# Tokenise, mix, route: the mixing loop of a three-stage model with router logits taken from unnormalised rows

## The reference, cut to what matters

```
h = tok(x)                                  # 16 sequences x 255 tokens x 256
h = h + attn(layernorm(h))                  # gated linear recurrence over tokens
h = h + ffn(layernorm(h))                   # 8 experts, top 1
# in ffn, with y = layernorm(h) (mean and variance over 256, eps 1e-5):
wg_n   = wg / max(norm(wg), 1e-4)
logits = (y @ w_red) @ wg_n.T               # 8 per token
gates  = softmax(logits); pick argmax; out = expert(y) * score
```

## Time and profile before

| what | value |
|---|---|
| median of 3 runs | 721.15 us (720.75 to 727.15) |
| the profiled execution | 719.72 us |
| its span | 718.0 us |
| PE, DVE, ACT, POOL busy | 86%, 67%, 33%, 29% of the span |
| mean granted TensorE clock | 0.905 of full |

### The profile page before, as it was taken

How to read it: one execution, slowest core, us unless ns; L and a number is a source line. 1 busy time by engine, 2 the same in 40 slices (tenths; PEclk the granted TensorE clock), 3 DMA queues, 4 the chain that set the end, 5 groups by cost and what they waited for, 6 DMA issues and landing times. The chain is left out here.

```text
span 718.0 us, 12918 instructions
## 1 busy us (share of the span) xinstructions
PE 614.3 (86%) x3301; PEld 397.0 (55%) x3302; DVE 481.7 (67%) x1258; ACT 239.5 (33%) x475; POOL 209.7 (29%) x293
## 2 busy tenths in 40 slices
PE   3989999999999999999619988899327999999993
PEld 3757776666677776666314444444113565665652
DVE  2568888888888888888658778784582444444441
ACT  2124444434434444434410222222202333333430
POOL 7322222222222222122111112121042455554532
PEclk8999999999999999999965779796556999999998
DMA  9101110111111100110012223211001212222210
GB/s 253 38 30 59 59 42 16 58 58 58 58 58 58 58 30 29 58 59 29 30 39 89 68 68 91 86 51 37 23 1 44 59 61 63 61 62 62 64 49 0
DMA packets 30309, 39.85 MB, mean 56 GB/s; under 512 B 5090, under 2 KB 21731, under 8 KB 30288
## 3 DMA queue, kind: packets, MB, share of 16 engines
q1 hardware_dynamic: 21712, 26.04, 12.0%
q0 software_dynamic: 3744, 9.34, 4.5%
q10 hardware_dynamic: 4832, 4.21, 1.9%
HBM read 30.92 MB, written 9.59 MB: 56 GB/s over the span
## 5 line engine op out<-in xcount | busy, mean ns | idle before, releaser
L465 PE MATMUL banks<-proj,xnT_h 128*128 128x512 f16 x384 | 114.4, 379 | 13.8 <-DVE early L1055 13.8
L1492 POOL TENSOR_TENSOR sm<-sm,minus_half 128x1 f32<-128x1 f32 x64 | 40.9, 639 | 124.7 <-DVE sm L1026 83.4
L465 PE MATMUL banks<-proj,xnT_l 128*128 128x512 f16 x192 | 72.8, 379 | 0.0
L465 PEld LDWEIGHTS banks<-proj,xnT_h 128*128 128x128 f16 x384 | 36.3, 98 | 55.9 <-DVE early L1055 17.6
L1391 DVE TENSOR_TENSOR vo<-banks,vo 128x256 f16<-128x256 f32 x39 | 16.6, 425 | 70.9 <-ACT vo L871 70.9
L1572 POOL DMA_INDIRECT out<-proj,vo x39 | 39.6, 1016 | 79.7 <-DVE vo L1408 79.7
L440 PE MATMUL banks<-early 128*128 128x256 f32 x256 | 62.0, 385 | 0.7 <-ACT early L728 0.7
L442 PE MATMUL banks<-early 128*128 128x256 f32 x256 | 60.5, 379 | 0.0
L1496 POOL TENSOR_TENSOR w1l<-stage,w1h 128x512 f32 (+1 forms) x16 | 18.5, 1156 | 140.6 <-ACT w1h L772 140.6
L671 PE MATMUL banks<-w2h,vo 128*128 x312 | 57.5, 273 | 1.2 <-DVE proj L1406 1.2
L651 PE MATMUL banks<-w1h,vo 128*128 x156 | 55.0, 394 | 3.2 <-ACT vo L877 2.1
(11 more groups left out here) (258 smaller groups left out, 1370.4 us busy)
## 6 DMA issues: line engine op xcount, KB each, us to landing
early<-in_x SPq DMA_DIRECT2D x16, 512.0 KB, 4.3
stage<-in_W SPq DMA_DIRECT2D x32, 256.0 KB, 2.8
early<-lam_by_chunk SPq DMA_DIRECT2D x32, 132.0 KB
token_rows<-rows ACTq DMA_DIRECT2D x16, 129.0 KB, 2.3
token_rows<-rows ACTq DMA_DIRECT2D x16, 112.9 KB, 1.9
early<-in_tok_W SPq DMA_DIRECT2D x2, 512.0 KB, 8.4
early<-lam_by_head SPq DMA_DIRECT2D x16, 64.0 KB
vo<-token_rows,vo POOLq DMA_INDIRECT x39, 2.9
```

The costliest lines, as they stand in the source:

```text
L465: last = mm(dst, a, c, start=(i == 0), stop=(i == n - 1))
L1492: ptt(sm[:, dst:dst + 1], sm[:, src:src + 1], minus_half[:], ALU.pow).then_inc(s["rstd_ready"], 1)
```

## The change

The router weights are centred in the prologue (one `bn_stats`, `bn_aggr` and subtraction on 16 partitions instead of a plain copy). In the mixing loop the residual sum goes to a ring `h2` of four rows of 258 instead of back into `rows`; PE transposes the unnormalised row and makes the logits with tokens on partitions, all 32 tiles side by side in bank 0; `normalise2`, `turn_logits`, `keep_logits` and `collect_logits` are gone. POOL does three operations for each tile (variance plus epsilon, and the power twice: once to `rstd2`, once behind the row). The routing starts with one multiplication of all logits by `rstd2`. The order of PE and of ACT inside a slot is changed as well, and the ring adds waits on the stores and transposes of four tiles earlier.

```diff
             def logits(t, w):
                 pe.wait_ge(s["t2_evac"], t + 1)
                 for c in range(DC):
-                    last = mm(banks[0:E, 0, 0:P], wrg[:, c, :], xT2[:, w, c * P:c * P + P], start=(c == 0), stop=(c == DC - 1))
+                    last = mm(banks[:, 0, bass.ds(t * E, E)], xT2[:, w, c * P:c * P + P], wrg[:, c, :],
+                              start=(c == 0), stop=(c == DC - 1))
                 last.then_inc(s["lg_ready"], 1)
...
-            def transpose_xn2(t, w):
-                pe.wait_ge(s["xn2_ready"], t + 1)
+            def transpose_h2(t, k):
+                pe.wait_ge(s["h2_done"], t + 1)
...
             def pair(p, ahead=True):
                 for k in range(4):
-                    mix(p, k)
+                    t = 4 * p + k
                     if ahead:
                         chunk_end(p + 1, k)
-                    t = 4 * p + k
-                    if not (isinstance(p, int) and t < 4):
-                        turn_logits(t - 4)
-                    if not (isinstance(p, int) and t < 3):
-                        logits(t - 3, (k + 1) % 2)
+                    mix(p, k)
                     if not (isinstance(p, int) and t < 2):
-                        transpose_xn2(t - 2, k % 2)
+                        logits(t - 2, k % 2)
+                    if not (isinstance(p, int) and t < 1):
+                        transpose_h2(t - 1, (k - 1) % 4)
...
-            with act.Fori(1, PAIRS) as p:
-                keep_ends(p)
+            def pair(p, first=False, ahead=True):
                 for k in range(4):
-                    collect_logits(4 * p + k - 4)
-                    keep_logits(4 * p + k - 3)
-                    keep_xT2(4 * p + k - 2, k % 2)
-                    store_rows(2 * p - 1 if k < 2 else 2 * p, k % 2)
+                    if k == 3 and ahead:
+                        keep_ends(p + 1)
+                    if not (first and k < 1):
+                        keep_xT2(4 * p + k - 1, (k - 1) % 2)
+                    if not (first and k < 2):
+                        store_rows(2 * p - 1 if k < 2 else 2 * p, k % 2, (k - 2) % 4)
...
                 copy(router_T[:, D:D + E], banks[0:16, 5, D:D + E]).then_inc(s["router_weights"], 1)
+                nc.vector.bn_stats(lst6[0:16], banks[0:16, 5, 0:D]).then_inc(s["router_centre"], 1)
...
+                nc.vector.bn_aggr(sm[0:16, 0:2], lst6[0:16]).then_inc(s["router_centre"], 1)
...
+                ts(router_T[:, 0:D], banks[0:16, 5, 0:D], sm[0:16, 0:1], None,
+                   ALU.subtract).then_inc(s["router_weights"], 1)
...
                 dve.wait_ge(s["out_ready"], t + 1)
-                tt(row[:, 0:D], bank(2 + k % 2, D), row[:, 0:D], ALU.add).then_inc(s["h2_done"], 1)
+                if not (isinstance(p, int) and p == 0):
+                    dve.wait_ge(s[f"table_in_{k}"], 16 * (1 + k % 2) * p)
+                    dve.wait_ge(s["t2_ready"], t - 3)
+                tt(h2[:, k, 0:D], bank(2 + k % 2, D), rows[:, bass.ds(t, 1), :].rearrange("p a b -> p (a b)"),
+                   ALU.add).then_inc(s["h2_done"], 1)
                 if left >= 4 and k == 3:
                     head_decays(p + 1)
-                if not (isinstance(p, int) and t == 0):
-                    normalise2(t - 1, (k + 1) % 2)
...
-                hsteps.step(nc.vector.bn_aggr(stats, lst6[:]))
+                hsteps.end()
+                nc.vector.bn_aggr(h2[:, k, D:D + 2], lst6[:]).then_inc(s["var2_ready"], 1)
                 if left >= 4:
                     Chunk(p + 1, k).spread()
-                hsteps.settle()
-                hsteps.step(ts(rstd, rstd, LN_EPS, None, ALU.add))
-                hsteps.end()
...
+            dve.wait_ge(s["rstd2_ready"], TILES)
+            tt(lg, bank(0, TILES * E).rearrange("p (t e) -> p t e", e=E),
+               wide(rstd2[:], T8), ALU.mult).then_inc(s["lg_scaled"], 1)
...
+            def root2(t, k, first):
+                if not first:
+                    pool.wait_ge(s["rstd2_ready"], apart(pool, t - 3))
+                var = h2[:, k, D + 1:D + 2]
+                pool.wait_ge(s["var2_ready"], t + 1)
+                ptt(eps_var[:, k:k + 1], var, ln_eps[:], ALU.add).then_inc(s["h2_eps"], 1)
+                pool.wait_ge(s["h2_eps"], apart(pool, t + 1))
+                ptt(rstd2[:, bass.ds(t, 1)], eps_var[:, k:k + 1], minus_half[:], ALU.pow)
+                ptt(var, eps_var[:, k:k + 1], minus_half[:], ALU.pow).then_inc(s["rstd2_ready"], 1)
```

More of the change, by code:

```diff
@@ L108, in build @@
         banks = ctx.enter_context(nc.psum_tensor("banks", [P, 8, 512], F32))
-        rows = sb("rows", [P, TILES, ROWC])
+        rows = sb("rows", [P, TILES, D])
         vo = sb("vo", [P, TILES, D])
@@ L131, in build @@
         minus_half = sb("minus_half", [P, 1])
+        ln_eps = sb("ln_eps", [P, 1])
+        eps_var = sb("eps_var", [P, 4])
+        rstd2 = sb("rstd2", [P, TILES])
         plus_half = sb("plus_half", [E, 1])
@@ L190, in build @@
         qst = sb("qst", [P, 2 * P])
-        lgT = early[0:E, 1536:1536 + P]
         lst = sb("lst", [P, D])
-        xn2 = xn
         xT2 = u
+        h2 = early[:, 4800:4800 + 4 * ROWC].rearrange("p (k c) -> p k c", k=4)
         flat = vo[:].rearrange("p t d -> p (t d)")
@@ L414, in multiply_router @@
             def multiply_router():
-                pe.wait_ge(s["router_weights"], 1)
+                pe.wait_ge(s["router_weights"], 2)
                 pe.wait_ge(s["wsplit_lo"], 8)
@@ L570, in transpose_xn2 @@
                 for c in range(DC):
-                    last = tr(bank(6)[:, c * P:c * P + P], xn2[:, w, c * P:c * P + P], ident[:])
+                    last = tr(bank(6)[:, c * P:c * P + P], h2[:, k, c * P:c * P + P], ident[:])
                 last.then_inc(s["t2_ready"], 1)
@@ L610, in _ @@
             pair(PAIRS - 1, ahead=False)
[L611 to L616, removed]
+            logits(TILES - 2, 0)
+            transpose_h2(TILES - 1, 3)
+            logits(TILES - 1, 1)
             pe.wait_ge(s["oh_ready"], 1)
@@ L823, in keep_xT2, with store_rows @@
                 af(xT2[:, w, :], bank(6, D), ACT.Copy).then_inc(s["t2_evac"], 1)
[L825 to L835, removed]
+            def store_rows(b, j, k):
+                act.wait_ge(s["rstd2_ready"], 2 * b + j + 1)
@@ L836, in store_rows @@
                 for start, stop in ((0, P),) if j == 0 else ((0, EVEN), (EVEN, NTOK - P)):
                     act.dma_start(token_rows[b, j * P + start:j * P + stop],
-                                  rows[start:stop, bass.ds(2 * b + j, 1), :].rearrange("p a b -> p (a b)")
-                                  ).then_inc(s["table_in"], 16)
+                                  h2[start:stop, k, :]).then_inc(s[f"table_in_{k}"], 16)
             keep_ends(0)
[L842 to L846, removed]
@@ L847, in _ @@
-            with act.Fori(1, PAIRS) as p:
-                keep_ends(p)
-                for k in range(4):
-                    collect_logits(4 * p + k - 4)
-                    keep_logits(4 * p + k - 3)
-                    keep_xT2(4 * p + k - 2, k % 2)
-                    store_rows(2 * p - 1 if k < 2 else 2 * p, k % 2)
[L854 to L858, removed]
@@ L864, in _ @@
+            pair(0, first=True)
+            with act.Fori(1, PAIRS - 1) as p:
+                pair(p)
+            pair(PAIRS - 1, ahead=False)
+            keep_xT2(TILES - 1, 1)
+            for j in range(2):
+                store_rows(B - 1, j, 2 + j)
             act.wait_ge(s["r_args"], 1)
@@ L960, in prologue_rest @@
                 dve.wait_ge(s["router_t"], 1)
-                copy(router_T, banks[0:16, 5, 0:D + E]).then_inc(s["router_weights"], 1)
+                copy(router_T[:, D:D + E], banks[0:16, 5, D:D + E]).then_inc(s["router_weights"], 1)
+                nc.vector.bn_stats(lst6[0:16], banks[0:16, 5, 0:D]).then_inc(s["router_centre"], 1)
+                dve.wait_ge(s["router_centre"], 1)
+                nc.vector.bn_aggr(sm[0:16, 0:2], lst6[0:16]).then_inc(s["router_centre"], 1)
+                dve.wait_ge(s["router_centre"], 2)
+                ts(router_T[:, 0:D], banks[0:16, 5, 0:D], sm[0:16, 0:1], None,
+                   ALU.subtract).then_inc(s["router_weights"], 1)
                 copy(colsum[:], bank(4, D))
@@ L1016, in normalise @@
                 lsteps.settle()
-                h = rows[:, bass.ds(t, 1), 0:D].rearrange("p a b -> p (a b)")
+                h = rows[:, bass.ds(t, 1), :].rearrange("p a b -> p (a b)")
                 stt(h, bank(2 + j, D), sm[:, 5:6], tokc, ALU.mult, ALU.add).then_inc(s["h_done"], 1)
@@ L1166, in _ @@
             split_v(B - 1)
-            hsteps = Steps(dve, s["h2_steps"], 3)
+            hsteps = Steps(dve, s["h2_steps"], 1)
             class Chunk:
@@ L1210, in head_decays @@
                 scan(qst[:], head_state_in[:], lam_head, 0.0, ALU.add, ALU.mult).then_inc(s["q_done"], 1)
[L1212 to L1220, removed]
             def slot(p, k, left):
@@ L1229, in slot @@
```

(17 more changed lines are left out.)

15 lines of the change are left out of this document (5 added, 10 removed).

## The result

The changed kernel takes 761.19 us (median of 4 runs, 760.31 to 761.55) against 720.95 us of the kernel before: ratio 1.058, 95% interval 1.0528 to 1.0631. It is slower by 40 us. The profiled execution has a span of 759.8 us, 41.8 more than before. Each ratio is taken over the runs within 1.5% of the fastest of their kernel, since single executions of some kernels come out several per cent longer. Beside the experiments the kernel before has medians of 723 to 726 us, so that a difference between two of the experiments, or between one and the changed kernel, is good to a few us only.

The account below looks back on a forecast made before the run. The prediction took a closed DVE-PE ring at clock 0.50 to bound the mixing loop, about 4.98 us a slot; routing 33.9 us later added to 719.72 gave 753.6, with 1.4 for the median 754, range 718 to 764.

Parts of the forecast that it names:

- The ring: Mixing loop: chunk_end before mix makes DVE and PE wait on each other every slot, 4.88 us unrolled, 4.98 in hardware loop.
- The clock: Mixing loop: PE's clock stays at 0.50 throughout, so slots take 4.9 to 5.0 us rather than 3.55.
- the form of PE's matmuls: New logits in the mixing loop: moving columns per instruction go from 128 to 8, so less moves through PE, at clock 0.50.
- The idle gaps: PE in the mixing loop: clock falls after a 1.93 us gap; at 1.00 each new slot would hold a 1.0 us gap.
- The first rival: Mixing loop: the clock comes and goes, half of 24 loop slots at 3.55 us; 736.6 us, 717 to 750; chance 0.20.
- the second: Mixing loop: clock at 1.00 from the fourth slot on despite 1.0 us gaps, slots 3.55 us; 712.0 us; chance 0.10.
- The sum: Terms from first residual add to routing: routing starts at 542.9 instead of 509.00, 33.9 us later.
- this case: Mixing loop at clock 0.50 throughout: 754 us, spread 749 to 759; chance 0.58.
- the third rival: Mixing loop: dearer logits, POOL or stores bind, slots 5.3 us in place of 4.98; 762 us, 759 to 768; chance 0.09.
- last add to routing: End of mixing loop: transpose 0.56, to logits 1.16, logits 1.02, to DVE 0.1, multiplication 0.46 us.
- What I costed at nothing: Router centring in the prologue, POOL's three operations, ACT's stores, waits on the ring of four rows, SP's loads: no cost.
- Covered, down to a slot of 2.5: Ring of four rows: stores of tile t-4 land in time for add(t) unless slots are shorter than 2.5 us.

Follow-up runs that it names:

- experiment 1: Changed kernel with PE's order undone, the mix of tile t ahead of chunk_end of chunk t+4 again: 731.22 us, 1.0139 of the kernel before.
- experiment 2: Kernel before with only PE's order changed, chunk_end ahead of the mix: 782.02 us, 1.0834 of the kernel before.
- experiment 3: Changed kernel plus one unread fp32 matmul of 256 moving columns (wide filler) in each PE slot with chunk work: 720.63 us, 0.9984 of before.
- experiment 4: Changed kernel plus two fp32 matmuls loading 128 weight columns but moving only 8 (narrow filler) in each slot with chunk work: 761.83 us, 1.0544 of before.
- experiment 10: Changed kernel with mix ahead of chunk_end and the logits matmul's operands exchanged, 128 columns moving (output wrong): 693.22 us, 0.9602 of before.
- experiment 7: Kernel before plus the filler of 256 moving columns in every slot: median 721.14 us against 723.1 for the kernel before beside it, ratio 0.9848.
- experiment 9: Kernel before with ACT's copy of lst moved to the pair's fourth slot: 698.45 us, 0.9675 of before.
- the half filler: Changed kernel with mix ahead of chunk_end and a filler of 128 moving columns in every slot: median 705.7 us, 693.5 to 723.6, ratio 0.9623.
- experiment 8: Changed kernel with DVE's waits on table_in and t2_ready moved ahead of the wait on out_ready: 757.8 us, 1.0494 of before.

## Why the prediction was right

**The ring, the step on which it rests, was right**, in mechanism and nearly in size. The slots ahead of the hardware loop are 4.87, 4.87 and 4.88 us against 4.88 from the earlier trace rows; L551 waits for `ends` by name 26 times; experiments 1 and 2 take the ring away and put it in, with -30 and +59 us and nothing else touched. It was a piece of luck that the old kernel's rows held the very chain, so that the sum could be read off.

**The clock, the step that was only argued, was right too**: it is at 0.50 from the first add to the last. Of the two reasons given, the form of PE's matmuls is the one that the experiments bear out: 3 and 4 add work of two forms to the same ring, 10 turns one matmul of experiment 1, none of them shortens the chain of waits, and the clock is at 1.00 with one form and at 0.50 with the other. The idle gaps were the weaker half: with gaps absent the clock stayed down (experiment 1), and with gaps of 1.2 us it stayed up (the profiled run of experiment 7). In the kernel before, PE has six gaps of 1.65 to 1.93 us that begin at full clock; at four of them it went to 0.50, by 0.7 us behind the gap's end at the latest, and at two it stayed at 1.00. One of those two, and the stretch behind it:

```profile
431.57 0.67 PE L563 MATMUL banks<-lst,qst 64*128 64x256 f32 x2 [1.75 <-ACT lst L817]
...
431.50:444.50 13.00, 11.28 (x53) 6.18 (x54) 11.98 (x42) 3.70 (x13) 3.23 (x4) 1.00 0.31 93
```

So "it falls after a gap", read from the one gap of the earlier trace rows, was too simple; that gap was also the longest of seven (1.06 to 1.93). With the gaps taken out, the clock of the profiled loop doesn't fall again once it is up (experiment 9). The first rival, a clock that comes and goes, is near to what the half filler does; the second, full clock in the ring, was built as experiment 3: I had 712.0 for it and it is 720.6, with slots of 3.65 to 3.85 for my 3.55, a filler in them and a tail of its own.

The Trainium skill (TensorE: Matmul & The Clock Gate, the section on why this matters for kernels) says that keeping TensorE busy without a break gets it past the throttle, and names gaps in which it is idle as what loses the clock again in mid-kernel. The windows of experiments 1 and 4 disagree: busy 20.00 and 19.69 of 20 us, clock 0.50. The busy column counts an instruction with 8 moving columns like one with 128: the four of a tile took 1.02 us at clock 0.50 in either form. The Trainium skill (Trainium Kernel Development and Optimization, Performance Expectations) calls matmul busy time a bad metric for how near a kernel is to its roof; here it is also a bad guide to the clock.

**The sum was short by 7.5 us** at the routing's start (33.9 forecast, 41.4 measured). The measured 761.2 us lies above the 749 to 759 that I gave this case and inside the 759 to 768 of the third rival; the range held it with 3 us to spare, by the room left for a rival whose reasons (dearer logits, POOL, stores) did not come true. I also added up wrongly at the end: 753.6 and 1.4 are 755, not 754. The terms:

| term | forecast | measured |
|---|---|---|
| first residual add | 387.08 | 388.66 |
| 27 slots with chunk work | 138.2 | 142.4 |
| of these, a slot in the hardware loop | 4.98 | 5.11 to 5.31 |
| what the head decays add | 0.68 | 0.53 (experiment 8: 5.65 - 5.12) |
| last four slots | 14.3 | 13.9 |
| last add to routing | 3.3 | 5.44 |

The first line: the first chunk's scan starts at 376.43 instead of 374.79, so that 1.6 of the 3.85 us were there before the loop began, and the ring made 2.2, as forecast (2.3). The 1.6 isn't the change's: the same scan starts between 374.65 and 377.81 in the thirteen traces kept, 374.79 to 377.81 in those built on the kernel before and 374.65 to 377.02 in those built on the changed one. As far as these traces show, it is chance. The hardware loop's slots: two waits that I had priced at nothing because their events come early, but which DVE must work off after the late one (experiment 8: 1.8 us over the slots), and 0.49 us from `ends` to L551 instead of 0.40 (0.09 a slot). The last line is a plain oversight: I counted one transpose and one logits behind the last add, while the order written out has logits, transpose, copy, logits. These rows are in the section on the profile after.

**What I costed at nothing** was at nothing, but for the handling of those two waits: all 32 adds waited for the mix, none for POOL or for the stores of the ring of rows. The centring of the router is covered in the prologue: DVE's wait for PE ahead of the copy of `wrg` is 2.06 us where it was 2.85. "Covered, down to a slot of 2.5" was roughly right and a little too bold: at slots of 2.3 to 3.3 us seven adds of experiment 10 wait for the stores.

**The gain that the change was in a position to have** went in two places: 30 us into the order of two calls, and 38 us into the direction of the logits matmul. Taking the copy of `lst` early, the one good part that I tried by itself, brings the old kernel to 698 us (experiment 9).

## What to carry to other kernels

When two engines hand work back and forth, write down for each wait which slot of the other engine it looks at, before and after an exchange of two calls: a wait whose producer is one slot back can close a ring, and the slot then costs the whole chain, however idle every engine is. When a matmul may be turned either way, look at the granted clock as well as at its duration: the form with few moving columns took the same time here and cost 38 us through the clock. And an idle PE beside a clock of 0.50 is a place to try a filler; it costs one line. Which filler matters: the wide one took 40 us off the changed kernel, the narrow one nothing, and in the kernel before the wide one changed nothing at the median (experiment 7).

## What was not expected of the hardware

PE was busy for 20.00 of 20 us in every window from 400 to 500 us at a granted clock of 0.50 (experiment 1). One fp32 matmul of 256 columns for each slot, whose result nobody reads, took the time from 761.2 to 720.6 us. POOL's addition on one element of each partition takes 0.70 us when it starts with DVE's scan and 0.19 when it doesn't:

```profile
442.77 0.70 POOL L1531 TENSOR_TENSOR eps_var<-early,ln_eps 128x1 f32<-128x1 f32 x1 [3.20 <-DVE early L1223]
442.78 0.70 DVE L1168 TENSOR_TENSOR_SCAN resp<-decay_in,early 128x264 f32<-128x264 f32 x1
...
448.46 0.19 POOL L1531 TENSOR_TENSOR eps_var<-early,ln_eps 128x1 f32<-128x1 f32 x1 [3.69 <-DVE early L1223]
```

The two lines at 442.77 and 442.78 are of the changed kernel's timeline, and so is the one at 448.46, where the scan began only at 448.84. It cost nothing here. The Trainium skill (GPSIMD Engine Reference, Specifications) says that POOL's memory interface is shared with VectorE and contended by DVE instructions with two inputs in SBUF; the scan is one, and these rows agree.
